# The first stage's modulation table in two column halves among the first weights, and the first block's other work in a new order

## The chip, the cores and the metric

The kernel runs on one core of one Trainium2 chip. The metric is the device time of one execution in microseconds, by the core's own clock; it includes loading all inputs from HBM and writing the output back.

## The reference, cut to what matters

The kernel is one adaptive-LayerNorm transformer block for 4 sequences of 1024 tokens of width 1024, all in float32.

```python
mod = (_silu(c) @ wmod).reshape(4, 6, 1, -1)          # table w_mod: 1024 x 6144
sa, ca, ga, sb, cb, gb = (mod[:, n] for n in range(6))
h = _layernorm(x) * (1 + ca) + sa
q = h @ wq_w + wq_b; k = h @ wk_w + wk_b; v = h @ wv_w + wv_b
x = x + ga * attention(q, k, v, wo_w, wo_b)
h = _layernorm(x) * (1 + cb) + sb
x = x + gb * routed_low_rank(h)
```

The first stage, `project`, computes the table product, the modulated h and q, k and v. Only the first two of the table's six column sections (sa, shift, and ca, scale) are needed before h can be formed; the other four are gates and the values for the second half, and are written to HBM for later stages.

## The kernel before, in words

`adaln_block` calls `project`, `attend` and `finish` one after the other. The change is inside `project`, and inside its first 512 tokens.

**Blocks and tiles.** `project` treats 8 blocks of 512 tokens. A block has 14 groups: 8 of q (g 0 to 7), 2 of k (8, 9), 4 of v (10 to 13). A group is 8 k-tiles (kt) of 128 rows, each of three matmuls, since both factors are split into a high part in fp32r and the rest (h_hi, h_lo, w_hi, w_lo). TensorE writes a group into one of four banks of `o_ps`; VectorE adds the bias and writes it into `side` (line 461 for q and k, 467 for v), ScalarE casts it to `o_hi` (342), GpSimd subtracts (`o_lo`, 372), SyncE stores both parts (272, 274).

**Preparing a block.** Half a block of x (256 tokens, 1 MB) is fetched (218), VectorE computes statistics and normalises it in place (405, 411, 420; ScalarE the root, 324), TensorE transposes it in 128-wide tiles into one of two banks of `t_ps` (525; one "turn" is one kt of one half), VectorE multiplies by 1 + scale and adds shift (`h_f`, 450), ScalarE casts to `h_hi` (335) and GpSimd subtracts to `h_lo` (363). While a block's groups run, the next block is prepared between them. The dictionary `PREPARE` says after which group each step stands, `MODULATE` the same for the rest of the table (`rows` loads four chunks, `mod` multiplies them). `events` makes one list of both, and every engine runs the same list in that order with its own part of each event. So the order of each engine's queue is written by hand.

**Before the first block.** The list `FIRST` is run ahead. The table's first two sections, 8 kt of 2048 columns, come in 16 chunks of 512 KB through the four slots of `stage` (234). For each kt, TensorE multiplies the two chunks with silu(c), repeated to 32 columns, as four products of 512 columns that lie in four row blocks of the one bank `m_ps` (498, `stage_used` up by 2). When all 16 chunks are in, VectorE copies the bank (426), TensorE turns it in four tiles (531), VectorE makes shift and scale (429, 431). Only then do w_q's chunks (512 KB each, line 250), split by ScalarE (`w_hi`, 315) and VectorE (`w_lo`, 437), and the tiles alternate: w_q kt, turn of both halves, and two kt later in the list the twelve matmuls of q groups 0 to 3 for that kt (`first_groups`, 509). The k and v weights (8 chunks of two loads, 252 and 253, `w_lo` on GpSimd, 352) stand at the end of `FIRST`, ahead of all of block 0, and x for the second block is fetched in their midst.

**Waits.** SyncE issues all loads and stores of the stage in program order. A chunk's load waits until the chunk four places before it has left its slot: for table chunks `stage_used`, for w_q `wq_lo_done`, for k and v `wkv_lo_done`. TensorE waits for group g - 4 to be taken before it writes g, and for h_f of the tile two before in the turn's bank.

## Time and profile before

| | |
|---|---|
| median of 3 runs | 3011.82 us (3004.32, 3011.96, 3011.82) |
| the profiled execution's own time | 3011.51 us |
| its span in the profile | 3009.7 us |
| TensorE matmul busy | 2894.5 us, 96% |
| VectorE, ScalarE, GpSimd busy | 1931.0 (64%), 1526.7 (51%), 1798.2 us (60%) |
| mean granted clock of TensorE | 0.976 of full speed |
| DMA, mean over the span | 80 GB/s; in the first 1/40 of it 229 GB/s |

The profile is one execution, seen by the hardware profiler. A page sums it up; views of the trace give the busy time in windows, single instructions in order of time with the idle time before them and what ended it, and groups of instructions. "0.73 <-DMA stage" behind an instruction means that its engine sat idle for 0.73 us until that transfer landed. The granted clock tells which share of its 2.4 GHz TensorE was given: 0.50 is 1.2 GHz. Matmuls are pipelined, so that one's duration overlaps the next; how long a row of them takes is read from their starts. The end of the last instruction and the kernel's own time differ by 1.8 us.

### The profile page before, as it was taken

How to read it: one execution, taken by the hardware profiler on the slowest of the kernel's cores; microseconds unless marked ns; L12 is line 12 of the kernel's file. 1: busy time of each engine (PE TensorE's matmuls, PEld its weight loads, DVE VectorE, ACT ScalarE, POOL GpSimd, SP SyncE). 2: the span in 40 equal slices, each digit the busy share in tenths (PEclk: the TensorE clock that was granted, in tenths of full speed). 3: DMA queues.
4: the chain of work that ended last, by engine and by line, in shares of the span. 5: the costliest groups of instructions: out<-in, count | busy, mean ns of one | idle time of the engine just before them, and what ended most of it. 6: DMA issues, size and time to landing. Idle time of an engine off the chain costs nothing. (4 is left out here: it accounts for less than half of the span.)

```text
span 3009.7 us, 49792 instructions
## 1 busy us (share of the span) xinstructions
PE 2894.5 (96%) x15590; PEld 1742.3 (58%) x15590; DVE 1931.0 (64%) x2572; ACT 1526.7 (51%) x2906; POOL 1798.2 (60%) x595
## 2 busy tenths in 40 slices
PE   6899999989999999999999999999999997999998
PEld 3687878874444444444444444444444435888886
DVE  3333333317777777777777777777777745766666
ACT  2111111105666666666666666666666662444444
POOL 2433333317888888888888888888888885211110
PEclk8899999998999999999999999999999998999998
DMA  6543334332211221221222122122212105333331
GB/s 229 172 137 124 129 131 137 129 116 84 56 45 43 55 51 36 55 51 42 49 51 52 39 51 55 39 48 55 51 36 55 41 12 165 96 110 107 108 105 63
DMA packets 156462, 241.61 MB, mean 80 GB/s; under 512 B 48992, under 2 KB 90400, under 8 KB 156320
## 3 DMA queue, kind: packets, MB, share of 16 engines
q1 hardware_dynamic: 156320, 240.05, 27.6%
q8 instruction: 48, 0.79, 0.1%
q14 instruction: 94, 0.77, 0.1%
HBM read 159.12 MB, written 79.82 MB: 79 GB/s over the span
## 5 line engine op out<-in xcount | busy, mean ns | idle before, releaser
L852 DVE TENSOR_REDUCE mx<-s_ps 128x1 f32<-128x1024 f32 x1024 | 1203.8, 1217 | 430.2 <-PE s_ps L921 423.5
L832 ACT ACTIVATE p_t<-st_ps 128x512 f32<-128x512 f32 x2048 | 1113.4, 595 | 553.3 <-PE st_ps L947 484.1
L790 POOL TENSOR_TENSOR p_sum<-p_sum,p_t 128x2048 f32<-128x2048 f32 x256 | 1173.3, 4583 | 22.1
L947 PE MATMUL st_ps<-q_st,k_st 98*128 98x512 f32 x2048 | 809.2, 435 | 11.3 <-ACT p_t L832 8.3
L947 PEld LDWEIGHTS st_ps<-q_st,k_st 98*128 98x128 f32 x2048 | 344.7, 187 | 604.3 <-ACT p_t L832 414.3
L921 PE MATMUL s_ps<-k_st,q_st 96*128 96x512 f32 x2048 | 657.9, 403 | 14.6 <-DMA q_st<-q_hi_d 10.9
L961 PE MATMUL num_ps<-p_t,v_sb 128*32 128x512 f32 x4096 | 546.1, 605 | 0.9 <-ACT p_t L832 0.9
L790 POOL TENSOR_TENSOR p_sum<-p_t 128x2048 f32<-128x2048 f32 x64 | 293.4, 4584 | 294.6 <-ACT p_t L832 294.6
L921 PEld LDWEIGHTS s_ps<-k_st,q_st 96*128 96x128 f32 x2048 | 389.6, 191 | 95.1 <-DVE mx L852 14.0
L372 POOL TENSOR_TENSOR o_lo<-side,o_hi 128x512 fp32r<-128x512 f32 x80 | 104.8, 1311 | 346.9 <-ACT o_hi L342 346.9
L1232 POOL TENSOR_TENSOR a_lo<-a_f,a_hi 128x1024 fp32r<-128x1024 f32 x32 | 76.1, 2379 | 358.9 <-ACT a_hi L1267 358.8
L557 PE MATMUL o_ps<-h_hi,w_hi 128*128 128x512 f32 x608 | 243.4, 400 | 2.5 <-issue 2.4
L557 PE MATMUL o_ps<-h_lo,w_hi 128*128 128x512 f32 x608 | 239.8, 394 | 0.0
L557 PE MATMUL o_ps<-h_hi,w_lo 128*128 128x512 f32 x608 | 239.7, 394 | 0.0
L461 DVE TENSOR_SCALAR side<-o_ps,bias_qk 128x512 f32<-128x512 f32 x80 | 59.9, 749 | 278.1 <-PE o_ps L557 275.6
L342 ACT CAST o_hi<-side 128x512 fp32r<-128x512 f32 x80 | 49.7, 621 | 356.9 <-DVE side L461 345.2
L1426 PE MATMUL o_ps<-wo_hi,a_hi 128*128 128x512 f32 x512 | 207.2, 405 | 13.9 <-POOL a_lo L1232 13.9
L1426 PE MATMUL o_ps<-wo_lo,a_hi 128*128 128x512 f32 x512 | 204.0, 398 | 0.0
L1426 PE MATMUL o_ps<-wo_hi,a_lo 128*128 128x512 f32 x512 | 203.7, 398 | 0.0
L1283 ACT ACTIVATE h_t<-t_ps,shift,scale 128x128 f32<-128x128 f32 x256 | 93.0, 469 | 162.1 <-PE t_ps L1492 162.1
L961 PEld LDWEIGHTS num_ps<-p_t,v_sb 128*32 128x32 f32 x4096 | 80.7, 108 | 129.6 <-issue 125.8
L363 POOL TENSOR_TENSOR h_lo<-h_f,h_hi 128x256 fp32r<-128x256 f32 x128 | 91.7, 739 | 100.2 <-ACT h_hi L335 100.2
(129 smaller groups left out, 2820.0 us busy)
## 6 DMA issues: line engine op xcount, KB each, us to landing
q_st<-q_hi_d SPq DMA_DIRECT2D x128, 256.0 KB, 4.4
stage<-w_mod SPq DMA_DIRECT2D x48, 512.0 KB, 5.3
...
att_d<-a_sb SPq DMA_DIRECT2D x128, 128.0 KB, 2.3
a_f<-att_d SPq DMA_DIRECT2D x32, 512.0 KB, 4.8
x_sb<-x SPq DMA_DIRECT2D x32, 512.0 KB, 5.4
```

Source lines behind the costliest of these rows:

```text
L363: nc.gpsimd.tensor_tensor(h_lo[:, 1 - par, kt, cols], h_f[:, bank_at(i, hf, kt), :], h_hi[:, 1 - par, kt, cols].bitcast(F32), ALU.subtract)\
L372: nc.gpsimd.tensor_tensor(o_lo[:, g % 2, :], o_f[:, g % 2, :], o_hi[:, g % 2, :].bitcast(F32), ALU.subtract)\
L557: last = nc.tensor.matmul(o_ps[:, bank, :], w[:, kt, g * P:(g + 1) * P], h[:, par, kt, :], start=begin, stop=end)
L790: nc.gpsimd.tensor_tensor(total, before, p_t[:, kt, :, :], ALU.add).then_inc(sum_done, 1)
L832: nc.scalar.activation(p_t[:, s, c, :], st_ps[:, c % 2, :], ACT.Exp, scale=SCALE)\
L852: nc.vector.tensor_reduce(mx[:, slot % 2, e:e + 1], s_ps[:, e % 2, :], AX_X, ALU.max)\
L921: part = nc.tensor.matmul(s_ps[:, e % 2, n * QW:(n + 1) * QW], q_st[0:STACK, slot, jj, t * P:(t + 1) * P], k_st[0:STACK, slot // 2, n * QW ...
L947: nc.tensor.matmul(st_ps[:, c % 2, :], k_st[:, slot // 2, s * P:(s + 1) * P], q_st[:, slot, jj, h * QW:(h + 1) * QW], start=True, stop=True)\
L961: last = nc.tensor.matmul(num_ps[c * HD:(c + 1) * HD, :], v_sb[:, slot // 2, s, :], p_t[:, s, c, :], start=s == 0, stop=s == NKT - 1)
L1232: nc.gpsimd.tensor_tensor(a_lo[:, u, :, :], a_f[:, u, :, :], a_hi[:, u, :, :].bitcast(F32), ALU.subtract).then_inc(a_lo_done, 1)
L1283: last = nc.scalar.activation(h_t[:, tt % 2, kt, :], t_ps[:, kt * P:(kt + 1) * P], ACT.Identity, bias=batch(shift2, bb)[:, kt:kt + 1], sca ...
L1426: last = nc.tensor.matmul(o_ps[:, u, cols], a[:, u, k, :], w[:, k, cols], start=(k == 0 and n == 0), stop=(k == KT - 1 and n == 2))
```

## The change

Four things move; no arithmetic changes except how the table's product is laid out.

- **The table in column halves.** A chunk is now one kt of both sections, but only 512 of each section's 1024 columns (128 partitions x 2 runs of 2 KB instead of one run of 4 KB). Eight chunks give the half c = 0, which holds shift and scale of kt 0 to 3; eight more give c = 1. Each chunk is multiplied as four products of 256 columns into half a bank: `m_ps` for c = 0, the new `m1_ps` for c = 1; the turned tiles go into the other half of the same bank. `shift` becomes two events.
- **The order of loads.** `RING` lists all chunks: 8 of the first half, then four times w_q of a kt and two chunks of the second half, then w_q of kt 4 to 7 and k, v weights. `load` gives each chunk its slot and its wait from this list.
- **k and v weights beside the groups.** Their splitting is taken out of `FIRST` and put after groups 1 to 4 of block 0 (`LATE`), two chunks at a time; the last four of their loads are issued there too. The fetch of the second block's x stands behind the loads of the first four.
- **Block 0 has dictionaries of its own.** `PREPARE_FIRST` has statistics after group 3 (was 0), turns after 5, 6, 7 and 10, 11, 12, up to three in a row (was after 2 to 5 and 9 to 12, two each); `MODULATE_FIRST` loads the first table rows after group 6 (was ahead of block 0) and multiplies them after 8 (was 3).

```diff
-    FIRST = [("stats", 0), ("norm", 0), ("stats", 1), ("norm", 1), ("shift",)]
+    PREPARE_FIRST = {-1: [("fetch", 0)], 3: [("stats", 0)], 4: [("norm", 0)],
+                     5: [("turn", 0, 0), ("turn", 0, 1), ("turn", 0, 2)],
+                     6: [("turn", 0, 3), ("turn", 0, 4), ("turn", 0, 5)],
+                     7: [("turn", 0, 6), ("turn", 0, 7), ("fetch", 1)], 8: [("stats", 1)], 9: [("norm", 1)],
+                     10: [("turn", 1, 0), ("turn", 1, 1), ("turn", 1, 2)],
+                     11: [("turn", 1, 3), ("turn", 1, 4), ("turn", 1, 5)],
+                     12: [("turn", 1, 6), ("turn", 1, 7)]}
+    MODULATE_FIRST = {6: [("rows", 0)], 8: [("mod", 0), ("rows", 1)], 11: [("mod", 1)]}
+
+
+    LATE = {1 + n // 2: [("w", KT + n - n % 2), ("w", KT + n - n % 2 + 1)] for n in range(KT)}
+
+
+
+    FIRST = [("stats", 0), ("norm", 0), ("stats", 1), ("norm", 1), ("modulate", 0), ("shift", 0)]
     for kt in range(KT):
+        if kt == KT // 2:
+            FIRST += [("shift", 1)]
         FIRST += [("w", kt), ("turn", 0, kt), ("turn", 1, kt)]
-    FIRST += [("w", KT + kt) for kt in range(KT)]
+        if kt >= 1:
+            FIRST += [("first", kt - 1)]
+        if kt < KT // 2:
+            FIRST += [("modulate", 1, 2 * kt), ("modulate", 1, 2 * kt + 1)]
+    FIRST += [("first", KT - 1)]
+
+
+    RING = [("mod", 0, kt) for kt in range(KT)]
+    for kt in range(KT // 2):
+        RING += [("w", kt), ("mod", 1, 2 * kt), ("mod", 1, 2 * kt + 1)]
+    RING += [("w", ch) for ch in range(KT // 2, 2 * KT)]
+
+    def slot_of(item):
+        return RING.index(item) % SLOTS
+
+    def loaded(item):
+
+        at = RING.index(item)
+        return sum(32 if e[0] == "w" and e[1] >= KT else 16 for e in RING[at % SLOTS:at + 1:SLOTS])
...
-    def events(prepare, modulate):
+    def events(prepare, modulate, first=False):
         seen = []
         for g in range(-1, NG):
             if g >= 0:
                 seen.append(("group", g))
+            if first:
+                seen += LATE.get(g, [])
+            if prepare:
+                seen += (PREPARE_FIRST if first else PREPARE).get(g, [])
             if modulate:
-                seen += MODULATE.get(g, [])
-            if prepare:
-                seen += PREPARE.get(g, [])
+                seen += (MODULATE_FIRST if first else MODULATE).get(g, [])
         return seen
...
+        do(0, 0, 0, events(True, True, True), 0)
...
+        m1_ps = ctx.enter_context(nc.psum_tensor("m1_ps", [P, 512], F32))
...
+                def load(item):
+                    at = RING.index(item)
+                    slot = at % SLOTS
+                    if at >= SLOTS:
+
+                        before = RING[at - SLOTS]
+                        if before[0] == "mod":
+                            sp.wait_ge(stage_used, before[1] * KT + before[2] + 1)
+                        elif before[1] < KT:
+                            sp.wait_ge(wq_lo_done, before[1] + 1)
+                        else:
+                            sp.wait_ge(wkv_lo_done, before[1] - KT + 1)
+                    if item[0] == "mod":
+                        half, kt = item[1:]
+                        src = w_mod_t[:, kt, 0:2 * D].rearrange("p (v c n) -> p v c n", v=2, c=2)[:, :, half]
+                        sp.dma_start(stage[:, slot, :].rearrange("p (v n) -> p v n", v=2), src)\
+                          .then_inc(stage_in[slot], 16)
+                    else:
+                        ch = item[1]
+                        rows = slice((ch % KT) * P, (ch % KT + 1) * P)
+                        if ch < KT:
+                            sp.dma_start(stage[:, slot, :], w_q[rows, :]).then_inc(stage_in[slot], 16)
+                        else:
+                            sp.dma_start(stage[:, slot, 0:NKV], w_k[rows, :]).then_inc(stage_in[slot], 16)
+                            sp.dma_start(stage[:, slot, NKV:2 * NKV], w_v[rows, :]).then_inc(stage_in[slot], 16)
+
+                for at, item in enumerate(RING[:-SLOTS]):
+                    if at == SLOTS:
                         fetch(0)
                         sp.dma_start(xn1, x[HALF:2 * HALF, :].rearrange("(t p) d -> p t d", p=P))\
                           .then_inc(x1_in, 16)
-                    if ch >= SLOTS:
...
+                    load(item)
+                fetch(2)
...
+                        elif ev[0] == "w":
+                            if ev[1] + SLOTS < W_CHUNKS:
+                                load(("w", ev[1] + SLOTS))
...
-
-                            dve.wait_ge(stage_used, MOD_CHUNKS)
-                            nc.vector.tensor_copy(o_f[:, 0, :], m_ps[:, :]).then_inc(mod_step, 1)
-                            dve.wait_ge(mod_step, 2)
-                            m = t_ps[:, 0, :].rearrange("p (c v j b r) -> p v j c b r", c=KT // 2, v=2, j=2, b=NB)
-                            nc.vector.tensor_copy(shift[:, :, :].rearrange("p (j c) b -> p j c b", j=2),
-                                                  m[:, 0, :, :, :, 0])
-                            nc.vector.tensor_scalar(scale1[:, :, :].rearrange("p (j c) b -> p j c b", j=2),
-                                                    m[:, 1, :, :, :, 0], 1.0, None, ALU.add).then_inc(mod_step, 1)
-                            dve.wait_ge(mod_step, 3)
+                            c = ev[1]
+                            m = (m_ps, m1_ps)[c]
+                            dve.wait_ge(stage_used, KT * (c + 1))
+                            nc.vector.tensor_copy(o_f[:, 0, c * HALF:(c + 1) * HALF], m[:, 0:HALF]).then_inc(mod_step, 1)
+                            dve.wait_ge(mod_step, 3 * c + 2)
+                            turned_m = m[:, HALF:2 * HALF].rearrange("p (c v j b r) -> p v j c b r", c=2, v=2, j=2, b=NB)
+                            tiles = slice(c * (KT // 2), (c + 1) * (KT // 2))
+                            nc.vector.tensor_copy(shift[:, tiles, :].rearrange("p (j c) b -> p j c b", j=2),
+                                                  turned_m[:, 0, :, :, :, 0])
+                            nc.vector.tensor_scalar(scale1[:, tiles, :].rearrange("p (j c) b -> p j c b", j=2),
+                                                    turned_m[:, 1, :, :, :, 0], 1.0, None, ALU.add).then_inc(mod_step, 1)
+                            dve.wait_ge(mod_step, 3 * c + 3)
...
-                            nc.vector.tensor_tensor(w_lo[:, ch, 0:D], stage[:, ch % SLOTS, :],
+                            nc.vector.tensor_tensor(w_lo[:, ch, 0:D], stage[:, slot_of(ev), :],
...
-                for kt in range(KT):
-                    for v in range(2):
-                        ch = 2 * kt + v
-                        pe.wait_ge(stage_in[ch % SLOTS], 16 * (ch // SLOTS + 1))
+                def modulate(c, kt):
+
+                    item = ("mod", c, kt)
+                    slot = slot_of(item)
+                    pe.wait_ge(stage_in[slot], loaded(item))
                     for j in range(4):
-                        last = nc.tensor.matmul(m_ps[32 * j:32 * j + 32, :], c_rep[:, kt, :],
-                                                stage[:, (2 * kt + j // 2) % SLOTS, (j % 2) * 512:(j % 2 + 1) * 512],
+                        last = nc.tensor.matmul((m_ps, m1_ps)[c][32 * j:32 * j + 32, 0:HALF], c_rep[:, kt, :],
+                                                stage[:, slot, j * HALF:(j + 1) * HALF],
                                                 start=kt == 0, stop=kt == KT - 1)
-                    last.then_inc(stage_used, 2)
+                    last.then_inc(stage_used, 1)
...
+                        elif ev == ("modulate", 0):
+                            for kt in range(KT):
+                                modulate(0, kt)
+                        elif ev[0] == "modulate":
+                            modulate(1, ev[2])
                         elif ev[0] == "shift":
-                            pe.wait_ge(mod_step, 1)
-                            for c in range(KT // 2):
-                                last = nc.tensor.transpose(t_ps[:, 0, c * P:(c + 1) * P],
-                                                           o_f[:, 0, c * P:(c + 1) * P], ident[:, :])
+                            c = ev[1]
+                            pe.wait_ge(mod_step, 3 * c + 1)
+                            for part in range(2):
+                                last = nc.tensor.transpose((m_ps, m1_ps)[c][:, (2 + part) * P:(3 + part) * P],
+                                                           o_f[:, 0, (2 * c + part) * P:(2 * c + part + 1) * P],
+                                                           ident[:, :])
                             last.then_inc(mod_step, 1)
-
-                            pe.wait_ge(mod_step, 3)
-                        elif ev[0] == "w":
-
-                            if 2 <= ev[1] <= KT + 1:
-                                first_groups(ev[1] - 2)
+                        elif ev[0] == "first":
+                            first_groups(ev[1])
```

Three places in the engines' queues. First SyncE, from the first table chunk to w_q; the engine's DMA instructions with what they wait for. Before:

```order
L234 DMA stage<-w_mod 128x1024 x4
L218 DMA xn<-x 128x2x1024
L229 DMA side<-x 128x2x1024
L234 DMA stage<-w_mod 128x1024 [waits stage_used] x12
L250 DMA stage<-w_q 128x1024 [waits stage_used] x4
L250 DMA stage<-w_q 128x1024 [waits wq_lo_done] x4
L252 DMA stage<-w_k 128x256 [waits wq_lo_done]
```

and in the changed kernel:

```order
L274 DMA stage<-w_mod 128x2x512 x4
L251 DMA xn<-x 128x2x1024
L288 DMA side<-x 128x2x1024
L274 DMA stage<-w_mod 128x2x512 [waits stage_used] x4
L280 DMA stage<-w_q 128x1024 [waits stage_used]
L274 DMA stage<-w_mod 128x2x512 [waits stage_used] x2
L280 DMA stage<-w_q 128x1024 [waits stage_used]
L274 DMA stage<-w_mod 128x2x512 [waits wq_lo_done]
L274 DMA stage<-w_mod 128x2x512 [waits stage_used]
L280 DMA stage<-w_q 128x1024 [waits stage_used]
L274 DMA stage<-w_mod 128x2x512 [waits wq_lo_done]
L274 DMA stage<-w_mod 128x2x512 [waits stage_used]
```

The load of the first w_q stands after 8 table chunks and no longer after 16; from there every third load is one of w_q, and each waits for the slot of another engine's work. The same pattern goes on to w_q of kt 3.

Second TensorE, from the table's last products to the tile of kt 1 (m_ps is the table's bank, side the copy of it or the second half of x, t_ps the banks of turned x). Before:

```order
L498 MATMUL m_ps<-stage,c_rep 32x512 [waits stage_in1,stage_in0]
L498 MATMUL m_ps<-stage,c_rep 32x512 x3
L498 MATMUL m_ps<-stage,c_rep 32x512 [waits stage_in3,stage_in2]
L498 MATMUL m_ps<-stage,c_rep 32x512 x3
L531 MATMUL t_ps<-ident,side 128x128 [waits mod_step]
L531 MATMUL t_ps<-ident,side 128x128 x3
L525 MATMUL t_ps<-ident,xn 128x128 [waits xn_ready,mod_step]
L525 MATMUL t_ps<-ident,xn 128x128
L525 MATMUL t_ps<-ident,side 128x128 [waits xn_ready]
L525 MATMUL t_ps<-ident,side 128x128
L525 MATMUL t_ps<-ident,xn 128x128 [waits h_ready,xn_ready]
```

and in the changed kernel, where both banks of the table are called m_ps:

```order
L542 MATMUL m_ps<-stage,c_rep 32x256 [waits stage_in3]
L542 MATMUL m_ps<-stage,c_rep 32x256 x3
L581 MATMUL m_ps<-ident,side 128x128 [waits mod_step]
L581 MATMUL m_ps<-ident,side 128x128
L569 MATMUL t_ps<-ident,xn 128x128 [waits xn_ready]
L569 MATMUL t_ps<-ident,xn 128x128
L569 MATMUL t_ps<-ident,side 128x128 [waits xn_ready]
L569 MATMUL t_ps<-ident,side 128x128
L542 MATMUL m_ps<-stage,c_rep 32x256 [waits stage_in1]
L542 MATMUL m_ps<-stage,c_rep 32x256 x3
L542 MATMUL m_ps<-stage,c_rep 32x256 [waits stage_in2]
L542 MATMUL m_ps<-stage,c_rep 32x256 x3
```

Two turned tiles in place of four stand ahead of the first turn of x, and eight products (two chunks) of the second half now stand between the turns of kt 0 and of kt 1, as they do again ahead of kt 2, 3 and 4.

Third VectorE, from the first group's bias of block 0. Before:

```order
L461 TENSOR_SCALAR side<-o_ps,bias_qk 128x512 [waits o_ready]
L405 BN_STATS stats<-xn 128x6 [waits x_in]
L405 BN_STATS stats<-xn 128x6 x3
L411 BN_AGGR mv<-stats 128x2 [waits ln_step]
L411 BN_AGGR mv<-stats 128x2
L461 TENSOR_SCALAR side<-o_ps,bias_qk 128x512 [waits o_ready]
L416 RECIPROCAL rstd<-std 128x2 [waits std_done]
L420 TENSOR_SCALAR xn<-xn,mv,rstd 128x1024 [waits ln_step]
L420 TENSOR_SCALAR xn<-xn,mv,rstd 128x1024
L461 TENSOR_SCALAR side<-o_ps,bias_qk 128x512 [waits o_lo_done,o_ready]
L450 TENSOR_SCALAR h_f<-t_ps,scale,shift 128x256 [waits h_lo_done,turned] x2
L461 TENSOR_SCALAR side<-o_ps,bias_qk 128x512 [waits o_lo_done,o_ready]
```

and in the changed kernel:

```order
L504 TENSOR_SCALAR side<-o_ps,bias_qk 128x512 [waits o_ready] x2
L504 TENSOR_SCALAR side<-o_ps,bias_qk 128x512 [waits o_lo_done,o_ready] x2
L446 BN_STATS stats<-xn 128x6 [waits x_in]
L446 BN_STATS stats<-xn 128x6 x3
L452 BN_AGGR mv<-stats 128x2 [waits ln_step]
L452 BN_AGGR mv<-stats 128x2
L504 TENSOR_SCALAR side<-o_ps,bias_qk 128x512 [waits o_lo_done,o_ready]
L457 RECIPROCAL rstd<-std 128x2 [waits std_done]
L461 TENSOR_SCALAR xn<-xn,mv,rstd 128x1024 [waits ln_step]
L461 TENSOR_SCALAR xn<-xn,mv,rstd 128x1024
L504 TENSOR_SCALAR side<-o_ps,bias_qk 128x512 [waits o_lo_done,o_ready]
L493 TENSOR_SCALAR h_f<-t_ps,scale,shift 128x256 [waits h_lo_done,turned] x3
```

All four first groups are taken before the statistics of the next x; normalising stands after group 4 in place of 1, and three tiles in a row stand behind group 5 where two stood behind groups 2 to 5. SyncE's and GpSimd's queues have k, v weights between those groups.

## Rows read from the trace of the kernel before

**Rows 1.** Windows: busy us of each engine, granted clock, DMA share and GB/s.

```profile
10.00:20.00 10.00, 3.53 (x20) 0.38 (x16) 4.81 (x10) 0.29 (x1) 0.00 (x0) 1.00 1.03 416
...
30.00:40.00 10.00, 5.80 (x24) 0.69 (x24) 0.19 (x1) 0.39 (x1) 0.00 (x0) 0.50 0.89 304
...
50.00:60.00 10.00, 10.00 (x48) 8.14 (x48) 5.62 (x9) 4.24 (x8) 3.15 (x5) 0.94 0.34 111
...
74.00:76.00 2.00, 0.90 (x4) 0.40 (x3) 0.69 (x2) 0.03 (x1) 2.00 (x3) 1.00 0.90 286
...
80.00:90.00 10.00, 3.80 (x28) 1.31 (x28) 5.17 (x7) 1.69 (x4) 5.23 (x4) 0.50 0.70 215
```

**Rows 2.** Timeline to 43 us: start, us, engine, line, operation, idle before and releaser.

```profile
22.39 1.82 PE L498 MATMUL m_ps<-stage,c_rep 128*32 128x512 f32 x8 [0.57 <-DMA stage<-w_mod]
...
23.02 1.53 DVE L420 TENSOR_SCALAR side<-side,mv,rstd 128x1024 f32<-128x1024 f32 x2
...
37.82 1.93 PE L498 MATMUL m_ps<-stage,c_rep 128*32 128x512 f32 x8 [1.84 <-DMA stage<-w_mod]
...
42.04 1.22 DVE L437 TENSOR_TENSOR w_lo<-stage,w_hi 128x1024 fp32r<-128x1024 f32 x1
```

**Rows 3.** Timeline of the first steps: cold matmuls, w_hi, w_lo, the last matmul.

```profile
45.70 0.80 PE L509 MATMUL o_ps<-h_hi,w_hi 128*128 128x512 f32 x1 [0.73 <-POOL h_lo L363]
...
50.57 0.63 PE L509 MATMUL o_ps<-h_lo,w_hi 128*128 128x512 f32 x1
...
60.01 1.05 ACT L315 CAST w_hi<-stage 128x1024 fp32r<-128x1024 f32 x1
...
61.09 1.23 DVE L437 TENSOR_TENSOR w_lo<-stage,w_hi 128x1024 fp32r<-128x1024 f32 x1 [1.43 <-ACT w_hi L315]
...
68.21 1.23 DVE L437 TENSOR_TENSOR w_lo<-stage,w_hi 128x1024 fp32r<-128x1024 f32 x1 [1.43 <-ACT w_hi L315]
...
74.51 0.39 PE L509 MATMUL o_ps<-h_lo,w_hi 128*128 128x512 f32 x1
```

**Rows 4.** DMA issues at 20, 52 and 70 us: count, KB each, us to landing.

```profile
stage<-w_mod SPq DMA_DIRECT2D x1, 512.0 KB, 3.9
...
stage<-w_q SPq DMA_DIRECT2D x1, 512.0 KB, 3.1
...
xn<-x SPq DMA_DIRECT2D x1, 1024.0 KB, 5.0
```

**Rows 5.** Timeline of TensorE after the first groups.

```profile
84.16 1.11 PE L525 MATMUL t_ps<-ident,xn 128*128 128x128 f32 x4 [9.26 <-DVE xn L420]
...
92.00 1.08 PE L573 MATMUL m_ps<-stage,c_rep 128*32 128x256 f32 x8 [1.45 <-DMA stage<-w_mod]
...
93.79 0.78 PE L557 MATMUL o_ps<-h_hi,w_hi 128*128 128x512 f32 x1
```

**Rows 6.** Timeline of block 0: VectorE takes the groups; TensorE's second table rows.

```profile
106.36 0.75 DVE L461 TENSOR_SCALAR side<-o_ps,bias_qk 128x512 f32<-128x512 f32 x1 [4.26 <-PE o_ps L557]
...
112.27 0.75 DVE L461 TENSOR_SCALAR side<-o_ps,bias_qk 128x512 f32<-128x512 f32 x1 [4.26 <-PE o_ps L557]
...
117.71 0.75 DVE L461 TENSOR_SCALAR side<-o_ps,bias_qk 128x512 f32<-128x512 f32 x1 [4.69 <-PE o_ps L557]
...
135.09 1.93 PE L573 MATMUL m_ps<-stage,c_rep 128*32 128x256 f32 x32
...
140.52 0.42 DVE L467 TENSOR_TENSOR side<-o_ps,bias_v 128x256 f32<-128x256 f32 x1 [0.31 <-PE o_ps L561]
...
143.82 0.42 DVE L467 TENSOR_TENSOR side<-o_ps,bias_v 128x256 f32<-128x256 f32 x1 [1.45 <-PE o_ps L561]
```

**Rows 7.** Groups of GpSimd, 0 to 330 us: count, busy us, mean ns, idle before.

```profile
L363 POOL TENSOR_TENSOR h_lo<-h_f,h_hi 128x256 fp32r<-128x256 f32 x70 | 50.2, 739 | 77.7 <-ACT h_hi L335 77.7
...
L372 POOL TENSOR_TENSOR o_lo<-side,o_hi 128x512 fp32r<-128x512 f32 x35 | 46.6, 1333 | 146.1 <-ACT o_hi L342 146.1
...
L352 POOL TENSOR_TENSOR w_lo<-stage,w_hi 128x512 fp32r<-128x512 f32 x8 | 10.0, 1271 | 0.1
```

32 lines of the change are left out of this document (4 added, 28 removed).

## The prediction

> **What bounds the kernel now.** I read the windows by stage first [rows 1]. TensorE is all but saturated from about 100 us on, so a change in the first stage pays only by what it takes out of the first 145 us. The last two columns to read there are the granted clock and the DMA rate: from 10 to 20 us the DMA engines move 416 GB/s, from 30 to 40 us only 304 GB/s with TensorE busy 5.80 of 10 us at clock 0.50, from 50 to 60 us TensorE is full at 0.94, and from 80 to 90 us it is busy only 3.80 us, at 0.50 again. There are therefore two holes. The timeline up to 43 us [rows 2] shows the first: normalised x is there at 24.55 us (23.02 plus 1.53), but the last table pair is multiplied only at 37.82, and the first w_lo and the first tile follow at 42.04. The timeline of the steady steps [rows 3] shows that each kt then takes 3.56 us ((68.21 - 61.09) / 2), a relay between ScalarE and VectorE, and that the first four groups end at 74.51 + 0.39 = 74.9 us. The second hole follows [rows 5]: TensorE waits 9.26 us for the second block's x, then multiplies table rows, and begins group 4 only at 93.79. After that the cadence is TensorE's own [rows 6], to the end of group 13 at about 143.8 us.
>
> **Part 1, table in column halves: -15.9 us at the first tile.** Eight chunks of 512 KB now hold all of the first four kt's shift and scale. In the kernel before, eight chunks are in when the fourth pair starts, 22.39 us [rows 2], the DMA engines being saturated until then [rows 1]; the same bytes come ahead now (four chunks, 2 MB of x, four chunks), so this time stands. A chunk's multiply costs 1.08 us cold (92.00, eight instructions of 256 columns, [rows 5]), so the sums are there at about 23.5, and VectorE is free at 24.55. From the end of the sums to the first w_lo it took 42.04 - 39.75 = 2.29 us: a copy, four turned tiles and two small operations. Half the columns and two tiles need about two thirds of it, 1.5: the first w_lo starts at about 26.1 instead of 42.04.
>
> **Part 2, the other half among the first steps: 4.8 us of it given back.** I follow the end of w_lo, kt by kt. Prices: a lone 512 KB load takes 3.1 us and one with another in flight 3.9 [rows 4]; w_hi 1.05 and w_lo 1.23 us [rows 3]; a kt's twelve matmuls about 5.2 us cold (eleven intervals from 45.70 to 50.57, the first the longest, [rows 3]) and 12 x 5.44 / 24 = 2.7 warm (a group of 24 takes 5.44, [rows 6]); a table chunk 1.08 cold [rows 5] and 1.93 / 4 = 0.48 warm [rows 6].
> kt 0: ends 27.3. kt 1: its w_q goes out when table chunk 7 is used (23.5), lands at 27.4 and costs nothing: 31.1. kt 2: its w_q needs the slot of a second-half chunk that TensorE uses only after the first turns, 29.0; it lands near 33.4, w_hi 34.5, w_lo ends 35.7, 1.0 us late. kt 3: TensorE does the first twelve matmuls, cold, from 30.2 to 35.3, and only then chunk 2 of the second half, 36.4; the queue is in order, w_q stands behind the table chunk that waits for this, goes out at 36.9 and lands at 41.1: w_lo ends 43.4, 4.1 us late. kt 4: the last two chunks land at 42.3 and 44.0, are used by 45.1, the second copy, turn and small operations take 1.3 us, so w_lo runs 46.4 to 47.6, 0.7 us late. kt 5 to 7 at 3.56 us: 58.3. The seven steps take 31.0 us; before they took 68.21 - 42.04 = 26.2, so 4.8 are given back. From the end of the last w_lo (69.44) to the end of the first groups it was 5.5 us; so these now end at **63.8 us, 11.1 us earlier**. I take the clock to rise about 36 us, some 10 us after TensorE is steadily in work: before it took from 45.70 to about 51 us (0.94 over the window from 50 us, [rows 1, 3]), but the work is thinner here. The two small turns, the second bank and eight semaphore waits lie inside these sums.
>
> The unknown here is the table's transfer in runs of 2 KB instead of 4 KB. No row shows such a load. Above, it is bounded by 416 GB/s [rows 1]; below, by k and v weights in runs of 1 KB, which reach 286 GB/s from 74 to 76 us while the queue issues them one by one [rows 1]. I take the upper value, since the two differ only in the run and the lower one is paced by its issues; at 286 GB/s each chunk costs 0.57 us more, the slot waits stretch, and the end moves to about 70. The Trainium skill (DMA: Bandwidth & Descriptors, section Bandwidth) says that loads from HBM are bound near 358 GB/s per core. By it, as an estimate, each of the twelve loads after 22 us would take 0.2 us more, of which about 1 us would reach the end; the 416 GB/s of the row speaks against it.
>
> **Part 3, preparation, table rows and k, v weights moved behind the groups: -12.6 us.** From 74.9 to 143.8 us the kernel before needs 68.9 us. Group 4 now starts at once: it needs group 0 taken, and VectorE no longer stands behind LayerNorm of the next x. TensorE's work there [rows 6]: six groups of 5.44 us (112.27 to 117.71), 32.6; two turned tiles cost 5.91 - 5.44 = 0.47, so sixteen cost 3.8; a v group with two tiles is 3.30 (140.52 to 143.82), so 2.85 alone and 11.4 for four; table rows two times 1.93, 3.9: together 51.7. Stalls I add:
> - Three tiles in a row have only two banks. The third waits for group 5's side (0.75 us, [rows 6]) and then the first tile's h_f: 1.0 us after group 5.
> - GpSimd between 63.8 and 82: o_lo of six groups at 1.33 and w_lo of eight chunks at 1.27, about 18 us in a row, queued ahead of the first h_lo (0.74) [rows 7]. VectorE's third h_f waits for that h_lo and group 6's side stands behind it, to about 83; TensorE's tiles after group 6 wait 1.5 us.
> - x for the second half is asked for after group 7's stores, about 93 us, and takes 5.0 [rows 4]; statistics until 101, norm until 107, just behind v group 10: 0.7 and 0.6 us; after group 11, 0.8 us.
> Sum 51.7 + 4.6 = 56.3; it ends at about 120.1. Costed at nothing: the eight k, v weight chunks, covered by group 4 to 7 (last w_lo about 80, first needed by group 8 at 90; without that cover their 10.2 us of GpSimd would stand open); the x load behind four weight loads at 60 us (needed by the statistics at 67); eight more switches between the 32-column and the full array, inside the 1.93 and 1.08 us of the rows.
>
> **Sum.** -15.9 + 4.8 - 12.6 = -23.7 us (143.8 to 120.1). Everything later is TensorE's cadence, moved as a whole. The profiled run took 3011.51 us (span 3009.7), the median of the runs shown is 3011.82: the forecast is 3011.5 - 23.7 = 2987.8, **2988 us**. The three runs lie 7.6 us apart, so I call no difference what is within 0.3% (9 us).
>
> **The rivals.**
> - **The clock rises early.** Before, TensorE was busy 58% of the time at 0.50 [rows 1]; now a 1.08 us multiply follows every 1.26 us (0.524 MB at 416 GB/s) until 23.5, and work goes on at 26. If the array runs at 2.4 instead of 1.2 GHz from 26 us on, the first twelve matmuls lose 2.4 us and two chunks 1.2, of which some 3 us reach the end: 2985. For it speaks that TensorE is busier, against it that the table multiplies are short and narrow. The Trainium skill (TensorE: Matmul & The Clock Gate, Part 1) states that idling halves the clock and sustained work restores it. By that rule the trace agrees: 1.00 from 74 to 76 us, then TensorE idles, and 0.50 from 80 us [rows 1].
> - **It stays cold, or the runs are slow.** If the clock rises only when the second half is through (50 us), four steps cost more and the first groups end at about 71; 286 GB/s would give nearly the same. Only about 4 us are left of part 1: 2995; both together give 3000.
> - **The second hole stays.** If x, norm or o_lo come late for the tiles after group 5, TensorE waits, cools and the gain of part 3 is given back: 3011.5 - 11.1 = 3000. For it: the 18 us GpSimd queue. Against: it is shorter than the groups that cover it.
> - **Slower: the ring becomes one chain.** Slots are freed in order, by three engines. If each kt waits for the previous one in full, a step costs two chunks (2.2), a load (3.9), w_hi and w_lo (2.3), the way from w_lo to the first matmul (45.70 - 43.27 = 2.4) and cold matmuls (5.2): 16.0 us instead of my 5.1, 44 us over four: 3031. It decides from 11.0 us a step. Against: four slots, and w_q is asked for two steps ahead.
> - **It does nothing**, because what is saved is waited for at attention's start: 3011. Against: nothing between 145 and 660 us waits for a fixed time.
>
> **How the numbers follow.** Forecast 0.57, early clock 0.17, cold or slow 0.12, second hole 0.07, chain 0.03, nothing 0.04. Likeliest: 2988. The range goes from the early clock with the runs' own spread below it (2979) to cold and slow together with the second hole's case (3001). Faster by over 0.3% (below 3002.8): 0.57 + 0.17 + 0.12 + 0.06 = 0.92; slower 0.03; same 0.05.
>
> **What would show it.** First h_f near 27 us; w_lo of kt 3 later than 3.56 us after kt 2's; the first groups ending at 62 to 66; no wait over 2 us on TensorE between them and group 13, which ends near 120; no clock of 0.50 between 80 and 90. I am wrong if the first tile is in time but the groups end after 71, if the profile shows a wait of TensorE for xn after group 5, or if the time between group 13 and the end differs from the 2865.9 us of before (3009.7 - 143.8) by over 5 us.

## The result, and the profile after

| | before | after |
|---|---|---|
| median | 3011.03 us (4 runs, 3004.32 to 3011.96) | 2969.82 us (4 runs, 2966.88 to 2975.26) |
| profiled execution, its span | 3011.51, 3009.7 us | 2971.44, 2969.6 us |
| mean granted clock | 0.976 | 0.985 |

The ratio is 0.987, 95% interval 0.9849 to 0.9891. The gain is 41 us; the forecast was 24 (2988 us), and the result lies 9 us below the lower end of the range. Four instants split both profiled executions: the first w_lo, the first group taken by VectorE, group 13 of block 0 taken, and the first score product of attention.

| us | before | after | change in the stretch |
|---|---|---|---|
| first w_lo | 42.04 | 27.64 | -14.4 |
| first group taken | 72.89 | 65.40 | +6.9 |
| group 13 taken | 143.82 | 125.46 | -10.9 |
| first score product | 672.3 | 632.6 | **-21.3** |
| end | 3009.7 | 2969.6 | -0.4 |

The last column is what the change does to the stretch that ends at this instant. Up to group 13 the change gives 18.4 us where 23.7 were forecast. The other 21.7 us come from behind it, where the forecast had nothing.

The first step after, timeline (start, us, engine, line, operation, idle before and releaser), to be read beside [rows 2, 3]:

```profile
24.27 1.08 PE L542 MATMUL m_ps<-stage,c_rep 128*32 128x256 f32 x8 [0.25 <-DMA stage<-w_mod]
...
24.70 1.54 DVE L461 TENSOR_SCALAR side<-side,mv,rstd 128x1024 f32<-128x1024 f32 x2
...
27.64 1.23 DVE L480 TENSOR_TENSOR w_lo<-stage,w_hi 128x1024 fp32r<-128x1024 f32 x1
...
32.42 1.23 DVE L480 TENSOR_TENSOR w_lo<-stage,w_hi 128x1024 fp32r<-128x1024 f32 x1 [2.65 <-ACT w_hi L356]
...
38.61 1.23 DVE L480 TENSOR_TENSOR w_lo<-stage,w_hi 128x1024 fp32r<-128x1024 f32 x1 [4.06 <-ACT w_hi L356]
...
43.91 1.23 DVE L480 TENSOR_TENSOR w_lo<-stage,w_hi 128x1024 fp32r<-128x1024 f32 x1 [3.17 <-ACT w_hi L356]
...
50.06 1.23 DVE L480 TENSOR_TENSOR w_lo<-stage,w_hi 128x1024 fp32r<-128x1024 f32 x1 [0.53 <-ACT w_hi L356]
```

The sums of the table's first half and the normalised x are ready together near 26 us, w_lo follows, and then four steps are longer than 3.56 us; the others keep it (53.61, 57.17, 60.73). The windows after (busy us of PE, PEld, DVE, ACT, POOL; granted clock; DMA share, GB/s), beside [rows 1]:

```profile
10.00:20.00 10.00, 4.15 (x32) 0.63 (x28) 3.13 (x8) 0.30 (x1) 0.00 (x0) 1.00 1.04 402
...
30.00:40.00 10.00, 9.91 (x52) 6.88 (x53) 3.52 (x5) 3.11 (x5) 2.66 (x4) 1.00 0.79 249
...
80.00:90.00 10.00, 8.61 (x40) 6.87 (x41) 2.95 (x6) 2.97 (x7) 9.37 (x11) 1.00 0.31 115
...
200.00:225.00 25.00, 25.00 (x139) 19.94 (x138) 10.15 (x17) 4.09 (x9) 7.99 (x8) 1.00 0.60 223
```

Both holes are closed: 9.91 us busy from 30 to 40 instead of 5.80, 8.61 from 80 to 90 instead of 3.80. The table comes at 402 GB/s though its runs are 2 KB; the Trainium skill (DMA: Bandwidth & Descriptors, Bandwidth) has loads from HBM bound near 358 GB/s, and in the same section 425 GB/s measured on one core alone. This row, of a kernel on one core, lies near the second and not the first. One column must not be trusted: the granted clock reads 1.00 throughout, yet eight table products take 1.08 us at 24.27 and 0.64 in a warm stretch. The durations show half speed until about 36.3 us (a product of 512 columns takes 0.63 us at 35.43 and 0.40 at 36.28), which is where the forecast had the rise.

In block 0 the GpSimd queue is as the forecast had it. Timeline of GpSimd and VectorE after:

```profile
66.88 2.54 POOL L413 TENSOR_TENSOR o_lo<-side,o_hi 128x512 fp32r<-128x512 f32 x2 [2.54 <-ACT o_hi L383]
...
84.04 1.28 POOL L413 TENSOR_TENSOR o_lo<-side,o_hi 128x512 fp32r<-128x512 f32 x1
85.28 1.42 POOL L404 TENSOR_TENSOR h_lo<-h_f,h_hi 128x256 fp32r<-128x256 f32 x2
...
86.12 0.54 DVE L493 TENSOR_SCALAR h_f<-t_ps,scale,shift 128x256 f32<-128x256 f32 x1 [5.37 <-POOL h_lo L404]
...
105.07 2.47 DVE L446 BATCH_NORM_STATS2 stats<-xn 128x6 f32<-128x512 f32 x4 [4.54 <-DMA xn<-x]
```

From 66.88 to 85.28 us GpSimd works 18.4 us in a row (forecast: about 18), and the third h_f comes at 86.12, 18.7 us after the end of the first groups at 67.4 (forecast: 19, from 63.8 to about 83).

**Where the other 21 us come from.** The diff has one more edit than the four that I described: `events` now appends `PREPARE` ahead of `MODULATE`, in every block. So the change isn't confined to the first 512 tokens, as I had written above. In the even blocks (2, 4, 6) both dictionaries have an entry ahead of the groups, the fetch of x and the first four table rows. Before, SyncE issued 2 MB of rows first and this x (the next block's) behind them. SyncE, VectorE and TensorE of the kernel before, in block 2, and its windows:

```profile
214.92 1.96 SPq L288 DMA_DIRECT2D stage<-w_mod  x4
...
217.18 0.38 SPq L218 DMA_DIRECT2D xn<-x  x1
...
226.91 2.47 DVE L405 BATCH_NORM_STATS2 stats<-xn 128x6 f32<-128x512 f32 x4 [6.88 <-DMA xn<-x]
...
233.23 1.11 PE L525 MATMUL t_ps<-ident,xn 128*128 128x128 f32 x4 [3.23 <-DVE xn L420]
...
234.57 0.63 PE L557 MATMUL o_ps<-h_hi,w_lo 128*128 128x512 f32 x1
...
220.00:245.00 25.00, 21.77 (x112) 16.81 (x111) 9.09 (x17) 3.66 (x8) 6.54 (x6) 0.86 0.39 145
```

and after:

```profile
196.33 0.40 SPq L251 DMA_DIRECT2D xn<-x  x1
...
197.01 2.17 SPq L329 DMA_DIRECT2D stage<-w_mod  x4
...
202.08 2.47 DVE L446 BATCH_NORM_STATS2 stats<-xn 128x6 f32<-128x512 f32 x4 [0.66 <-DMA xn<-x]
```

Before, x lands 9.7 us after its issue (226.91 - 217.18) and VectorE waits 6.88 for it; TensorE then waits 3.23 us and afterwards runs at half speed for a time (0.63 us for a product of 512 columns instead of 0.39). After, x lands in 5.8 us, and TensorE is busy 25 of 25 us at the upper level. Read from the distances between x's fetches, the old order costs 6.34, 6.32 and 4.25 us in the three blocks, 16.9 in all. The forecast read block 0 closely and took all later blocks for TensorE's own cadence.

The last 4.4 us lie at a branch. The blocks run in a loop of two (an odd and an even one), and at the first of its two jumps back TensorE of the kernel before waits for nothing that the view names:

```profile
293.11 0.28 PE L561 MATMUL o_ps<-w_hi,h_lo 128*128 128x256 f32 x1
295.83 0.49 PE L557 MATMUL o_ps<-h_hi,w_hi 128*128 128x512 f32 x1 [2.44 <-issue]
...
297.13 0.63 PE L557 MATMUL o_ps<-h_lo,w_hi 128*128 128x512 f32 x1
...
300.11 0.55 PE L557 MATMUL o_ps<-h_hi,w_hi 128*128 128x512 f32 x1
```

After 2.44 us of idle time it works a little at full speed, then about 3 us at half. The stretch that holds this takes 75.9 us from the fetch of a second half to the next such fetch, against 71.7 after; the one that holds the second jump takes 71.9 against 71.7. Together: 18.4 + 16.9 + 4.4 + 0.4 = 40.1 us, the difference of the two spans.

### The profile page after: what moved, and what is told of

It is laid out like the page before. It is cut to its first block and busy times, and to the rows that moved or that the text cites. A ratio compares the mean times of both kernels' runs of the same rounds, so it can differ in the third digit from the quotient of the medians.

```text
span 2969.6 us, 49916 instructions
## 1 busy us (share of the span) xinstructions
PE 2880.7 (97%) x15654; PEld 1735.6 (58%) x15654; DVE 1931.5 (65%) x2575; ACT 1526.4 (51%) x2906; POOL 1798.1 (61%) x595
## 5 line engine op out<-in xcount | busy, mean ns | idle before, releaser
L837 POOL TENSOR_TENSOR p_sum<-p_sum,p_t 128x2048 f32<-128x2048 f32 x256 | 1173.2, 4583 | 22.1
L968 PE MATMUL s_ps<-k_st,q_st 96*128 96x512 f32 x2048 | 657.6, 403 | 14.7 <-DMA q_st<-q_hi_d 11.0
```

The costliest lines, as they stand in the source:

```text
L837: nc.gpsimd.tensor_tensor(total, before, p_t[:, kt, :, :], ALU.add).then_inc(sum_done, 1)
L968: part = nc.tensor.matmul(s_ps[:, e % 2, n * QW:(n + 1) * QW], q_st[0:STACK, slot, jj, t * P:(t + 1) * P], k_st[0:STACK, slot // 2, n * QW ...
```

## The experiments

All instants below are from the profiled execution of each kernel; "to scores" is the distance from group 13 taken to the first score product; "x late" is what blocks 2, 4 and 6 take beyond the kernel after, by SyncE's fetches of x (after: 109.3 us from group 13 to the second fetch of block 2, and 71.7 us each for blocks 4 and 6); "branch" gives the two times between such fetches that hold the loop's jump back, ahead of blocks 3 and 5.

| kernel | first w_lo | first group | group 13 | to scores | x late, sum | branch |
|---|---|---|---|---|---|---|
| before | 42.04 | 72.89 | 143.82 | 528.5 | 16.9 | 75.9, 71.9 |
| after | 27.64 | 65.40 | 125.46 | 507.2 | 0 | 71.7, 71.7 |
| order alone | 42.20 | 72.92 | 142.56 | 510.4 | 0.0 | 73.4, 73.5 |
| order undone | 26.45 | 61.74 | 121.69 | 518.8 | 10.7 | 71.9, 71.9 |
| halves alone | 26.61 | 63.83 | 135.98 | 519.2 | 10.9 | 71.9, 71.9 |
| block 0 alone | 41.94 | 71.73 | 131.56 | 530.4 | 14.7 | 76.0, 75.8 |
| fetch first | 42.22 | 73.06 | 144.16 | 507.8 | 0.1 | 71.9, 71.9 |
| padded | 46.75 | 77.65 | 148.11 | 531.2 | 17.9 | 74.1, 75.4 |
| filler | 26.30 | 62.91 | 127.12 | 507.7 | 0.0 | 71.7, 71.7 |
| rows behind x | 26.62 | 61.11 | 121.83 | 508.0 | 0.8 | 71.7, 71.7 |
| turns first | 42.27 | 71.86 | 141.28 | 524.8 | 14.5 | 73.4, 73.6 |
| x first | 27.98 | 64.02 | 123.59 | 507.4 | 0.0 | 71.7, 71.7 |

**1. The order alone.** The kernel before with the two steps swapped:

```diff
-            if modulate:
-                seen += MODULATE.get(g, [])
             if prepare:
                 seen += PREPARE.get(g, [])
+            if modulate:
+                seen += MODULATE.get(g, [])
```

> The kernel before with one edit: in every block, blocks 0, 2, 4 and 6 among them, each group's preparation events stand ahead of its table events, so x is fetched before the four table rows at a block's start. Theory A (the 21.7 us that the change gains behind group 13 of block 0 are the x load that no longer queues behind 2 MB of table rows in blocks 2, 4 and 6): about 3011 - 22 = 2989 us, all of it behind 144 us in the trace, TensorE without a wait for xn in those blocks, 7 us less in each. Rival B (they come from block 0's own new order, which leaves the queues in another phase): no change, 3011 us.

2995.6 us (2992.73 to 2997.62) against 3011.96; ratio 0.9944 (0.9927 to 0.996), -16.4 us. "To scores" falls by 18.1. Theory A holds, but with 22 us it was too large by 6: the late x goes (16.9 us), while TensorE still stands idle at both branches (1.41 and 1.57 us). The swap is a part of its own, worth 16 us where the whole forecast was 24.

**2. The order undone.** The changed kernel, with the old order in all blocks but the first:

```diff
-            if prepare:
-                seen += (PREPARE_FIRST if first else PREPARE).get(g, [])
-            if modulate:
-                seen += (MODULATE_FIRST if first else MODULATE).get(g, [])
+            steps = [(PREPARE_FIRST if first else PREPARE).get(g, []) if prepare else [],
+                     (MODULATE_FIRST if first else MODULATE).get(g, []) if modulate else []]
+            for step in (steps if first else steps[::-1]):
+                seen += step
```

> The changed kernel with the order of the two kinds of events put back in all blocks but the first. Theory A: 2970 + 22 = 2992 us, with the wait of TensorE for xn and the clock of 0.5 back in blocks 2, 4 and 6; block 0 unchanged, its group 13 taken near 125.5 us. Rival B: stays at 2970 us.

2979.81 us (2975.75 to 2983.47); ratio to before 0.9893 (0.9874 to 0.9911): 10 us over the changed kernel, where A said 22 and B none. The late x costs only 10.7 us here against 16.9 before, and no stall at the branch comes back with it. So the price of the old order is not a constant: in blocks 2, 4 and 6 TensorE waits 2.81, 2.05 and 2.12 us for the normalised x (before: 3.23, 3.82, 2.67) and runs 7, 0 and 8 products of 512 columns at half speed afterwards (before: 11, 9, 5), each of which costs 0.20 us (starts 0.43 instead of 0.23 us apart).

**3. The halves alone.** The changed kernel with k, v weights back in `FIRST` (and their loads back ahead of block 0, x fetched in their midst; not shown) and the old dictionaries and order throughout:

```diff
+    FIRST += [("w", KT + kt) for kt in range(KT)]
...
-            if first:
-                seen += LATE.get(g, [])
-            if prepare:
-                seen += (PREPARE_FIRST if first else PREPARE).get(g, [])
             if modulate:
-                seen += (MODULATE_FIRST if first else MODULATE).get(g, [])
+                seen += MODULATE.get(g, [])
+            if prepare:
+                seen += PREPARE.get(g, [])
```

> The table in column halves with its ring, but k and v weights at the end of the list as before, block 0 with the dictionaries of before, and the old order of events. My terms for parts 1 and 2 say that the first groups end 11.1 us earlier; the changed kernel's trace shows 7.6 (67.3 for 74.9). If the parts add up: 3011 - 7.6 = 3003 us, with the first hole as in the changed kernel and the second hole (9 us for xn) as before. Rival: the second hole swallows it, since what it waits for (x behind k, v weights) starts no earlier: 3008 to 3011.

2992.03 us (2988.31 to 2995.28); ratio 0.993 (0.9912 to 0.9948), -20 us, where 3003 us was expected, or 3008 to 3011 by the rival. The start gives 7.8 us at group 13, about what was expected (7.6). The second hole does not swallow it: TensorE waits 9.26 us there, exactly as before, but earlier. The rest comes behind group 13: 6.0 us less of the late x (TensorE's waits are 2.20, 2.75 and 2.29 us, with 7, 5 and 0 slow products behind them) and 4.0 at the branch. Nothing in the edit acts there by design; experiment 6 asks about the branch.

**4. Block 0's new order alone.** The kernel before (whole table) with `LATE`, `PREPARE_FIRST` and `MODULATE_FIRST`, and the loads moved with them:

```diff
-    FIRST += [("w", KT + kt) for kt in range(KT)]
+        if kt >= 1:
+            FIRST += [("first", kt - 1)]
+    FIRST += [("first", KT - 1)]
...
+            if first:
+                seen += LATE.get(g, [])
+                seen += PREPARE_FIRST.get(g, [])
+                seen += MODULATE_FIRST.get(g, [])
+                continue
```

> The table whole as before; k, v weights beside groups 1 to 4, preparation and table rows of block 0 by the new dictionaries, old order of events in the other blocks. My term for part 3 was 12.6 us, the changed kernel's trace shows 68.9 - 58.1 = 10.8. If the parts add up: 3011 - 10.8 = 3000 us, first groups at 74.9 as before, group 13 taken near 133. Rival: without the early start the x load is no longer behind and more is gained, 2998.

3002.53 us (2999.02 to 3003.71); ratio 0.9967 (0.9953 to 0.9981), -9.4 us. Group 13 comes 12.3 us earlier, close to the 12.6 forecast for this part: 1.2 of it by the first group, since the first groups of a kt now stand one kt earlier in the list, and 11.1 between that and group 13. 1.9 are lost behind it, where both blocks with the branch now take 76 us.

**5. Only the fetch first, and 9. only the turns first.** The two halves of the swap in the kernel before. The first swaps the steps ahead of the groups (x's fetch and table rows), the second those behind groups (turns and table arithmetic):

```diff
-            if modulate:
-                seen += MODULATE.get(g, [])
-            if prepare:
-                seen += PREPARE.get(g, [])
+            steps = [MODULATE.get(g, []) if modulate else [], PREPARE.get(g, []) if prepare else []]
+            for step in (steps[::-1] if g < 0 else steps):
+                seen += step
```

```diff
-            for step in (steps[::-1] if g < 0 else steps):
+            for step in (steps[::-1] if g >= 0 else steps):
```

> The kernel before, with x fetched ahead of the four table rows at the two points of an even block where both stand (blocks 2, 4 and 6), but with the table's arithmetic still ahead of the turns behind groups 3 and 11. A: the gain of the order is that the fetch of x no longer waits behind 2 MB of table rows: then the time is that of the order alone, about 2995 us (16 us under the kernel before), the distance from group 13's eviction to the first score product is about 510 us as with the order alone, against 528.5, and no wait of TensorE of over 1 us for the turned x stands between 120 us and 590 us. B: it is the order of table arithmetic and turns on VectorE, GpSimd and TensorE's queue that matters: then the time stays within 4 us of 3011, the distance at 525 us or more, and VectorE's turned-x evictions still come behind the table's.

> The kernel before, with the turns of x put ahead of the table's arithmetic behind groups 3 and 11 of the even blocks, and with x fetched behind the table rows as before: the other half of the swap. A: only the order of the fetch counts: then the distance from group 13's eviction to the first score product stays at 525 to 532 us, VectorE's waits for x of 6 to 7 us in blocks 2, 4 and 6 stay, and the time is within 4 us of 3011. B: the turns' place pays too: then TensorE's waits for the turned x in those blocks fall from 3 to 4 us each to under 2.5, the distance is 515 to 522 us, and the time 3001 to 3006; with both halves additive, fetch order and this would have given over 20 us in the kernel with the order alone, which gave 16.

Fetch first: 2993.06 us (2989.63 to 2994.9), ratio 0.994 (0.992 to 0.996), -18.1 us. Turns first: 3010.27 us (3004.99 to 3014.03), ratio 0.9989 (0.9979 to 1.0). The timelines of block 2, fetch first and then turns first:

```profile
215.26 0.39 SPq L217 DMA_DIRECT2D xn<-x  x1
215.94 2.18 SPq L287 DMA_DIRECT2D stage<-w_mod  x4
...
221.04 2.47 DVE L404 BATCH_NORM_STATS2 stats<-xn 128x6 f32<-128x512 f32 x4 [0.67 <-DMA xn<-x]
...
215.00:240.00 25.00, 25.00 (x139) 19.90 (x138) 10.24 (x17) 4.21 (x9) 6.98 (x7) 1.00 0.60 206
```

```profile
212.16 1.96 SPq L287 DMA_DIRECT2D stage<-w_mod  x4
214.41 0.38 SPq L217 DMA_DIRECT2D xn<-x  x1
...
223.91 2.47 DVE L404 BATCH_NORM_STATS2 stats<-xn 128x6 f32<-128x512 f32 x4 [6.65 <-DMA xn<-x]
...
230.23 1.11 PE L524 MATMUL t_ps<-ident,xn 128*128 128x128 f32 x4 [3.00 <-DVE xn L419]
...
220.00:245.00 25.00, 22.00 (x118) 17.22 (x118) 9.31 (x16) 3.65 (x8) 6.65 (x7) 0.93 0.42 150
```

With the fetch first no wait of TensorE of over 0.2 us is left between group 13 and the scores. This settles it: the fetch ahead of 2 MB of rows is, within the runs' spread, the whole gain of the swap (theory A of both; of turns first, "to scores" at 524.8 lies just below A's band, by shorter lateness), and the place of the turns is worth 0 to 6 us by its interval (0.9979 to 1.0), 1.6 by the medians.

**6. The stall at the branch: padded.** The kernel before with 18 small products at the start, read by nobody:

```diff
+                for n in range(18):
+                    nc.tensor.matmul(t_ps[:, 0, 0:8], ident[:, :], ident[:, 0:8], start=True, stop=True)
```

> The kernel before with 18 matmuls of 8 columns more at the start of TensorE's stream: some 2 us of work at a time when TensorE has nothing else to do. A: the stall of 1.4 to 2.5 us at the turn of the loop (released by nothing that the profile shows, with some columns at half clock behind it) depends on where the loop's instructions lie in memory, and 18 instructions more shift it away, as the halves do, which also lengthen the stream by 18: then both turns of the loop take 72.0 us as without the stall (before: 75.9 and 72.0 in one profile), and the time is 3 to 8 us under 3011. B: the stall belongs to the whole-width table or to the data of the block behind it: then it stays, one of the two turns takes 75 us or more, and the time is within 2 us of 3011.

3016.28 us (3013.79 to 3019.84); ratio 1.0015 (1.0004 to 1.0027). A falls: TensorE stands idle at both branches (2.00 and 1.94 us); the second:

```profile
451.30 0.49 PE L559 MATMUL o_ps<-h_hi,w_hi 128*128 128x512 f32 x1 [1.94 <-issue]
```

The loss of 5.1 us (3016.28 against 3011.14) was in neither theory. I had written "some 2 us" for the padding; TensorE took

```profile
8.56 7.85 PE L493 MATMUL t_ps<-ident 128*128 128x8 f32 x36 [8.56 <-DVE c_rep L390]
16.34 3.64 PE L500 MATMUL m_ps<-stage,c_rep 128*32 128x512 f32 x16
...
46.75 1.23 DVE L437 TENSOR_TENSOR w_lo<-stage,w_hi 128x1024 fp32r<-128x1024 f32 x1
```

7.85 us, the four slots of the ring stayed full for 6.8 us longer, and the first w_lo came 4.7 us later, the first group 4.8, group 13 4.3. By accident it shows that a delay ahead of the first step passes on nearly whole.

What goes with the stall is in the DMA queues of the same traces, which list packets of the kind `instruction` apart. In the kernel before, queue 8 brings such packets, 16 KB each, at 291.06, 292.93 and 297.02 us, around the idle time that ends at 295.83; from 434 to 560 us it brings none, and at the second branch in there (447.4) TensorE is not held up. In the changed kernel there is none from 272 to 560 us. The queues of before from 290 to 298 us, of block 0 alone from 430 to 437 (second branch, 2.46 us idle) and of order alone from 428 to 434 (1.57 us idle):

```profile
q8 instruction: 3, 0.05, 2.6%
...
q8 instruction: 3, 0.05, 3.1%
...
q8 instruction: 2, 0.03, 2.2%
```

and all that is listed from 434 to 560 us before, and from 272 to 560 us after:

```profile
q1 hardware_dynamic: 14960, 16.81, 40.0%
...
q1 hardware_dynamic: 34211, 40.10, 41.7%
```

The twelve profiles hold 24 such branches, two each. At nine TensorE is idle for 1.41 to 2.53 us (the first of before, both of order alone, block 0 alone, padded and turns first), and at each of these a packet of queue 8 starts 2.65 to 3.44 us before TensorE's next product. At the other fifteen the idle time is at most 0.07 us, and no such packet starts in the 6 us before. So the stall goes with instructions being fetched at the branch. No experiment set the fetching on or off, so that this is an agreement in all 24 cases, and not a cause shown by an edit.

**7. The early clock.** The changed kernel with idle turns of the identity tile between the first half's products:

```diff
+                                for n in range({3: 22, 7: 5}.get(kt, 1)):
+                                    nc.tensor.transpose(t_ps[:, n % 2, 0:P], ident[:, :], ident[:, :])
```

> The changed kernel with idle turns of the identity tile (127 columns' worth each, read by nobody) between the first half's table products, so that TensorE is busy without gaps from the first chunk to the last of that half. A: with the engine busy the clock stands at its upper level before the first weight eviction: table products of the second half take 0.63 to 0.70 us for a chunk of eight instead of 1.08, pairs of turns 0.44 instead of 0.69, the first groups' evictions come 1 to 3 us earlier than at 65.4, and the time is 2966 to 2970. B: the first groups are paced by the weights' evictions and by VectorE, whatever TensorE's level: then the first group's eviction stays within 0.7 us of 65.4 and the time within 1.5 us of 2969.8.

2970.52 us (2966.88 to 2974.71), the changed kernel's time. The clock did rise early, as the first turns show (0.44 us for a pair; after, 0.69):

```profile
25.53 0.44 PE L583 MATMUL m_ps<-ident,side 128*128 128x128 f32 x2 [0.56 <-DVE side L468]
25.81 0.38 PE L569 MATMUL t_ps<-ident,xn 128*128 128x128 f32 x2
```

but the first group is taken at 62.91, within the 61.1 to 65.4 of the kernels that load in this order. Its clock even fell later, to 0.93 and 0.90 from 70 to 90 us, behind a wait of 2.17 us for xn (after: 0.95), and from the first group to group 13 it takes 64.2 us against 60.1. So what this execution may have won at the start it lost there. B holds for the time: the edit as a whole pays nothing that can be measured. The intervals of both kernels are 6 us and more to each side, so a gain of 3 us is neither shown nor excluded.

**8. Block 0's rows behind x**, as in the even blocks:

```diff
-    MODULATE_FIRST = {6: [("rows", 0)], 8: [("mod", 0), ("rows", 1)], 11: [("mod", 1)]}
+    MODULATE_FIRST = {7: [("rows", 0)], 9: [("mod", 0), ("rows", 1)], 12: [("mod", 1)]}
```

> The changed kernel with block 0's table rows asked for one group later, behind the x of the next half, as in the other even blocks. A: VectorE's wait of 4.5 us for x at 105.07 us goes, the turned x of block 1 is not late, and group 13's eviction comes 1 to 3 us earlier than 60.1 us after the first group's: 2967 to 2969. B: the wait is cover that nobody waits for, or another wait takes its place: group 13's eviction stays within 0.5 us of 60.1 us after the first group's and the time within 1.5 us of 2969.8.

2971.31 us (2967.63 to 2972.61). VectorE's wait is halved, and TensorE waits for the rows instead:

```profile
98.56 2.47 DVE L446 BATCH_NORM_STATS2 stats<-xn 128x6 f32<-128x512 f32 x4 [2.35 <-DMA xn<-x]
...
102.62 0.64 PE L620 MATMUL m_ps<-stage,c_rep 128*32 128x256 f32 x8 [0.76 <-DMA stage<-w_mod]
104.04 0.64 PE L620 MATMUL m_ps<-stage,c_rep 128*32 128x256 f32 x8 [0.77 <-DMA stage<-w_mod]
```

From the first group to group 13 it takes 60.7 us against 60.1, just outside B's 0.5 us, and the time is B's.

**10. x ahead of the first four table chunks**, in the changed kernel:

```diff
-                    if at == SLOTS:
+                    if at == 0:
```

> The changed kernel with both fetches of x ahead of the first four table chunks in SyncE's queue. A: the norm of block 0's x (VectorE busy to within 0.3 us of the first half's table eviction) sets the first weight eviction: x lands 2 to 3 us earlier, the table chunks 2 us later; the end of the table's first half then sets it, at 26 to 28 us, no earlier than the 26.45 to 27.64 of the three profiles of this start: time within 2 us of 2970. B: SyncE's issues and the ring are not what binds the chunks: then the table is not late, the first weight eviction comes at 24.5 to 25.5 us, the first group's at 60 to 61 us and the time is 2966 to 2968. C: the chunks' landings all slip behind x: first weight eviction at 28.5 us or later, time 2972 or more.

2971.6 us (2969.24 to 2972.35). The norm is done 5.8 us earlier than after, and VectorE waits for the table:

```profile
18.87 1.54 DVE L461 TENSOR_SCALAR side<-side,mv,rstd 128x1024 f32<-128x1024 f32 x2
26.49 0.42 DVE L468 COPY side<-m_ps 128x256 f32<-128x256 f32 x1 [6.08 <-PE m_ps L542]
```

The first w_lo starts at 27.98. A holds: the sum of the bytes ahead of it (2 MB of x, 4 MB of table) sets it, whichever comes first. Of the variants of the changed kernel none is measurably faster than it.

## Why the prediction was wrong

**The failed step** is "Everything later is TensorE's cadence, moved as a whole". It was costed at nothing and is worth -21.3 us in the profiled execution, 16.9 by x's fetch ahead of the table rows in blocks 2, 4 and 6 (experiments 1 and 5) and 4.4 at the branch. The step failed in the reading of the diff, not of the hardware: the swap stands there, and I listed four edits and priced four. Its premise, that TensorE is all but saturated from about 100 us on and a change can pay only in the first 145, was wrong with it. The trace of before had the sign of it too, a wait of VectorE for x of 6.88 us and granted clock 0.86 from 220 to 245 us. My own test of the forecast (2865.9 us from group 13 to the end, wrong if off by over 5) gives 2844.1. Without what came behind group 13 the 18.4 us would have made 2993 us, inside the range.

**Part 1** (-15.9) was right: -14.4 in the profiled execution, -15.4 to -15.7 in the four others that load in this order (experiments 2, 3, 7, 8).

**Part 2** (4.8 given back) was mis-sized in the profiled execution, where it is 6.9, but 3.6 to 6.4 in the other four (what the stretch from the first w_lo to the first group takes beyond the 30.85 us of before). The mechanism holds, steps longer than 3.56 us while the second half comes. The forecast put the delay on kt 3; steps 1 to 4 took 4.8, 6.2, 5.3 and 6.2 us, spread over all. In the two SyncE rows below, the same four issues at the same place take 3.44 us after and 2.12 us in "rows behind x", and with it x is issued 1.3 us later and the first w_lo starts 1.0 us later:

```profile
3.08 3.44 SPq L274 DMA_DIRECT2D stage<-w_mod  x4
```

```profile
3.08 2.12 SPq L274 DMA_DIRECT2D stage<-w_mod  x4
```

With them the first group is taken at 65.40 and at 61.11 us, though both kernels are the same up to there. The other 3.3 us are spread over the next four steps, and no run shows what sets them. So of the 5.3 us by which the part up to group 13 fell short (18.4 instead of 23.7), up to 4 are this one execution: order undone, with the same block 0, has group 13 at 121.69, 22.1 us earlier than before.

**Part 3** (-12.6) measured -10.9 in the pair of profiles and, counted the same way from the first group, -11.1 alone in experiment 4. Stalls of TensorE there were 4.7 us (2.6 for h_f, 2.1 for xn) against 4.6 forecast. One of them, 0.95 us for xn right behind group 5, was not in the forecast, which had named such a wait as a sign of being wrong; it is too short to matter. The later runs confirm the place named, GpSimd's 18 us in a row.

**Unknown cost, runs of 2 KB:** 402 GB/s, so the value taken (the upper) was right.

**The rivals.** The early clock was tested: its 3 us do not show at the end (2970.52 against 2969.82 us), which the runs' spread does not exclude. It did not happen by itself: TensorE worked at half speed until 36.3 us. Staying at half speed, the second hole and the single chain did not happen (steps of 4.8 to 6.2 us, 11.0 needed for the chain). "It does nothing" fell, and experiment 6 shows a shift of the start arriving nearly whole. None of the rivals held a gain behind group 13, so the range could not hold the result.

**What stays open** is why the stall at the branch is there in one kernel and not in another. It stands at nine of the twelve branches of the six kernels with the whole table ("fetch first" has none) and at none of the twelve with the halves, and 36 rows more in TensorE's stream did not remove it. The Trainium skill (Runtime: NRT & Kernel Launch, Instruction fetch mechanics) says that a taken branch whose target is not at hand stalls the engine until it is fetched. The idle time agrees, and so do the packets of instructions beside each of the nine (experiment 6). But no run here shows why some kernels fetch instructions in every pass of the loop and others do not.
